# Four residual layers on one core: the down projection's rank products, moved into gate and up chunk by chunk and spread over the array's columns

## The reference, cut to what matters

```python
def lora_add(base, inp, A, B):                  # one adapter of rank 16 per batch
    t = einsum('bri,bni->bnr', A[idx], inp)
    return base + einsum('bor,bnr->bno', B[idx], t) * 0.5
gate = lora_add(einsum('bnh,fh->bnf', x, W_gate), x, A_gate, B_gate)     # f = 1376
up   = lora_add(einsum('bnh,fh->bnf', x, W_up),   x, A_up,   B_up)
act  = silu(gate) * up
down = lora_add(einsum('bnf,hf->bnh', act, W_down), act, A_down, B_down)
x = x + down
```

## Time and profile before

| | |
|---|---|
| time, median of 3 runs | 320.55 us (319.75 to 320.6) |
| profiled execution, its own time | 319.52 us |
| its span | 317.7 us |
| TensorE matmuls busy | 309.4 us (97%) |
| VectorE, ScalarE, GpSimd busy | 153.2, 107.0, 20.1 us |
| granted TensorE clock, mean | 0.999 |

### The profile page before, as it was taken

The page is one execution under the profiler, slowest core; times in us unless marked ns, Lnnn a source line. Parts: engine busy times, 40 slices in busy tenths (PEclk is TensorE's granted clock), DMA queues, the critical chain, the costliest instruction groups (busy, mean ns, idle before and its releaser), DMA issues.

```text
span 317.7 us, 4612 instructions
## 1 busy us (share of the span) xinstructions
PE 309.4 (97%) x1672; PEld 256.3 (81%) x1672; DVE 153.2 (48%) x250; ACT 107.0 (34%) x164; POOL 20.1 (6%) x25
## 2 busy tenths in 40 slices
PE   6879999999999999999999999999999999999996
PEld 5358788988888888888888888888889788897886
DVE  0198997967669437254254254255624431111101
ACT  1276562504445346243243243245325220000000
POOL 2086400200100000000000000000000000000000
PEclk9999999999999999999999999999999999999999
DMA  5989981015203400431431421550632002110111
GB/s 170 340 298 356 366 287 41 0 38 170 59 2 124 140 2 0 133 101 34 132 99 34 132 99 33 166 148 0 193 121 93 0 0 66 35 33 2 46 53 35
DMA packets 23888, 33.21 MB, mean 105 GB/s; under 512 B 3264, under 2 KB 16064, under 8 KB 23744
## 3 DMA queue, kind: packets, MB, share of 16 engines
q1 hardware_dynamic: 23584, 32.48, 32.0%
q10 hardware_dynamic: 288, 0.52, 0.5%
HBM read 30.89 MB, written 2.10 MB: 104 GB/s over the span
## 4 chain that ended last, share of the span: by engine, by line
PE 92%; SPq 3%; DMA 3%; POOL 1%; issue 1%; DVE 0%
PE bank L956 24%; PE bank L957 24%; PE bank L958 24%; PE bank L1101 3%; PE bank L1057 3%; DMA aw_raw<-in_aw 3%; PE bank L910 3%; PE bank L1003 2%; PE bank L940 1%; PE bank L890 1%; PE bank L942 1%; PE bank L941 1%; PE bank L932 1%; SPq L324 1%; SPq L304 1%; PE bank L1124 1%
## 5 line engine op out<-in xcount | busy, mean ns | idle before, releaser
L956 PE MATMUL bank<-xb,wgu_hl 128*128 128x512 f32 x176 | 69.1, 392 | 0.0
L957 PE MATMUL bank<-xb,wgu_hl 128*128 128x512 f32 x176 | 69.0, 392 | 0.0
L958 PE MATMUL bank<-xb,wgu_hl 128*128 128x512 f32 x176 | 68.5, 389 | 0.0
L958 PEld LDWEIGHTS bank<-xb,wgu_hl 128*128 128x128 f32 x176 | 33.1, 188 | 7.2
L815 DVE TENSOR_TENSOR act_f<-bank,act_f 128x512 f32<-128x512 f32 x22 | 15.2, 691 | 48.9 <-PE bank L1057 47.2
L956 PEld LDWEIGHTS bank<-xb,wgu_hl 128*128 128x128 f32 x176 | 33.0, 188 | 5.8
L957 PEld LDWEIGHTS bank<-xb,wgu_hl 128*128 128x128 f32 x176 | 33.2, 189 | 5.3
L956 PE MATMUL bank<-act_hl,wd_hl 128*128 128x512 f32 (+1 forms) x99 | 36.6, 370 | 0.0
L957 PE MATMUL bank<-act_hl,wd_hl 128*128 128x512 f32 (+1 forms) x99 | 36.2, 366 | 0.0
L958 PE MATMUL bank<-act_hl,wd_hl 128*128 128x512 f32 (+1 forms) x99 | 36.2, 366 | 0.0
L421 ACT ACTIVATE act_hl<-act_f 128x512 f32 (+1 forms) x22 | 13.9, 632 | 61.7 <-DVE act_f L815 61.6
(11 more groups left out here) (127 smaller groups left out, 450.5 us busy)
## 6 DMA issues: line engine op xcount, KB each, us to landing
w_raw<-in_w SPq DMA_DIRECT2D x22, 256.0 KB, 7.5
wgu_raw<-in_wgu SPq DMA_DIRECT2D x11, 512.0 KB, 3.4
bgu_raw<-in_bgu SPq DMA_DIRECT2D x88, 64.0 KB, 2.2
w_raw<-in_w SPq DMA_DIRECT2D x7, 512.0 KB, 7.4
out<-x_f SPq DMA_DIRECT2D x7, 256.0 KB, 2.4
x_f<-in_xT SPq DMA_DIRECT2D x6, 256.0 KB, 7.5
wd_own<-in_wd SPq DMA_DIRECT2D x2, 704.0 KB, 4.9
wd_raw<-in_wd SPq DMA_DIRECT2D x2, 704.0 KB, 4.3
```

Of the source, the lines that this page charges most:

```text
L956: pe.matmul(dst, w_hi, x[0][:, cols], start=start, stop=False)
L957: pe.matmul(dst, w_hi, x[1][:, cols], start=False, stop=False)
L958: return pe.matmul(dst, w_lo, x[0][:, cols], start=False, stop=stop)
```

## The change

The rank products of the down projection no longer form a block behind gate and up. `down_ranks(fc)` now does one chunk of both halves: for each half, four matmuls, one per batch, of plain float32 weights (`ad_raw`, 16 columns, no split) by plain float32 values (`act_f`, 128 columns), batch j of the half into partitions 32j to 32j+15 of bank h, which are the array's output columns from 32j on. Chunk fc-1 is done inside chunk fc, between gate and up of half 0, and the last chunk after the first piece of the down projection. The sums over chunks accumulate in bank 0 and bank 1, of which DVE first sets 128 columns to zero.

So the splitting of `ad`, `td_uv` and its splitting, and the two L1134 matmuls go. `td_copy` copies the banks' 128 columns to `td_sb`, and `spread_ranks(h)` makes two plain float32 matmuls of 128 columns with a selecting matrix `td_sel`, which POOL builds. ScalarE's silu of a chunk now also waits (`td_tm`) until the rank products of the chunk before have read `act_f`. `ad_raw` is loaded much earlier, into the place of layer 2's `a2_hl`. TensorE's loop over chunks 1 to 10 is written out. In the down projection the order of pieces and of the splits around them is new: both spreads stand after the second piece.

```diff
-        ad_raw = at("ad_raw", o_act + 80 * KB, [B, FC, R])
-        ad_hl = at("ad_hl", o_ad, [B, FC, 2, R], F32R)
+        ad_raw = at("ad_raw", o_ad, [B, FC, R])
         td_st = at("td_st", o_slot2 + 4 * KB, [T], F32R)
-        td_uv = [at(f"td_uv{i}", o_slot2 + 2 * i * KB, [HT], F32R) for i in range(H)]
+        td_sb = at("td_sb", o_ad + 8 * KB, [H, S])
+        td_sel = at("td_sel", o_ad + 9 * KB, [2, P])
...
+            sp.wait_ge(l2_tm, 2)
+            for b in range(B):
+                sp.dma_start(ad_raw[:, b], ad[adapter3[b]]).then_inc(ad_in, 16)
...
+            pool.memset(td_sel[:], 0.0).then_inc(td_sel_step, 1)
+            pool.wait_ge(td_sel_step, 1)
+            pool.wait_ge(sel_in, 16)
+            for j in range(HB):
+                rows = slice(32 * j, 32 * j + 32)
+                first = 64 * (j % 2)
+                pool.tensor_copy(td_sel[rows, j // 2, first:first + 64],
+                                 sel_raw[rows, 3 * P:3 * P + 64]).then_inc(td_sel_step, 1)
+            pool.wait_ge(td_sel_step, 1 + HB)
...
-            def td_uv_high(h):
-                act.wait_ge(td_tm, h + 1)
-                high(td_uv[h][0:2 * R], bank[h][0:2 * R]).then_inc(td_uv_hi, 1)
+            def td_copy(h):
+                act.wait_ge(td_tm, 2 * FC - 1 + h)
+                high(td_sb[:, h], bank[h][:, 0:S]).then_inc(td_copied, 1)
...
                         if h == 0:
                             act.wait_ge(act_lo, 2 * fc - 1)
+                            act.wait_ge(td_tm, 2 * fc - 1)
                         else:
                             act.wait_ge(act_lo, 2 * fc)
+                            act.wait_ge(td_tm, 2 * fc)
...
             act.wait_ge(up_done, 2 * FC)
             down_split_hi("wd_1")
             down_split_hi("bd")
-            act.wait_ge(act_lo, 2 * FC)
-            td_uv_high(0)
+            td_copy(0)
+            td_copy(1)
             down_split_hi("wd_2")
             td_high(0)
+            td_high(1)
             down_split_hi("wd_3")
-            td_uv_high(1)
...
+            def zero_td_bank(h):
+
+                dve.wait_ge(t3_uv_lo, h + 1)
+                dve.memset(bank[h][:, 0:S], 0.0).then_inc(td_banks_zeroed, 1)
...
             down_split_lo("bd")
-            td_uv_low(0)
             down_split_lo("wd_2")
             td_low(0)
+            td_low(1)
             down_split_lo("wd_3")
-            for i in range(C):
-                x3_add(i)
-            td_uv_low(1)
-            td_low(1)
-            for i in range(C, len(DOWN_PIECES)):
+            for i in range(len(DOWN_PIECES)):
                 x3_add(i)
 
 
...
-            with pe.Fori(0, (FC - 1) // 2) as i:
-                for u in range(2):
-                    fc = 2 * i + 1 + u
-                    slot = 1 - u
-                    pe.wait_ge(wgu_lo, fc + 1)
-                    pe.wait_ge(bgu_ready, fc + 1)
-                    for h in range(H):
-                        pe.wait_ge(silu_done, 2 * fc - 1 + h)
-                        gate_up_main(0, h, slot)
-                        gate_up_lora(0, h, slot)
-                        pe.wait_ge(act_mul, 2 * fc - 1 + h)
-                        gate_up_main(1, h, slot)
-                        gate_up_lora(1, h, slot)
-
-
-            def down_ranks(h):
-
-                pe.wait_ge(act_lo, 2 * FC - 1 + h)
-                for j in range(HB):
-                    b = HB * h + j
-                    for f in range(FC):
-                        for k in range(2):
-                            ins = pe.matmul(bank[h][0:2 * R, j * S:(j + 1) * S],
-                                            ad_hl[:, b, f].rearrange("p k r -> p (k r)"),
-                                            act_hl[:, f, k, b * S:(b + 1) * S],
-                                            start=(f == 0 and k == 0), stop=(f == FC - 1 and k == 1))
-                ins.then_inc(td_tm, 1)
+
+            def down_ranks(fc):
+
+                for h in range(H):
+                    pe.wait_ge(act_mul, 2 * fc + h + 1)
+                    for j in range(HB):
+                        ins = pe.matmul(bank[h][32 * j:32 * j + R, 0:S], ad_raw[:, HB * h + j, fc],
+                                        act_f[h][:, j * S:(j + 1) * S], start=(fc == 0), stop=(fc == FC - 1))
+                    ins.then_inc(td_tm, 1)
+
+            pe.wait_ge(ad_in, 16 * B)
+            pe.wait_ge(td_banks_zeroed, H)
+            for fc in range(1, FC):
+                slot = fc % 2
+                pe.wait_ge(wgu_lo, fc + 1)
+                pe.wait_ge(bgu_ready, fc + 1)
+                for h in range(H):
+                    pe.wait_ge(silu_done, 2 * fc - 1 + h)
+                    gate_up_main(0, h, slot)
+                    gate_up_lora(0, h, slot)
+                    if h == 0:
+                        down_ranks(fc - 1)
+                    pe.wait_ge(act_mul, 2 * fc - 1 + h)
+                    gate_up_main(1, h, slot)
...
+            def spread_ranks(h):
+
+                pe.wait_ge(td_copied, h + 1)
+                for q in range(2):
+                    ins = pe.matmul(bank[2 + h][:, q * S:(q + 1) * S], td_sel[:, q], td_sb[:, h], start=True,
+                                    stop=True)
+                ins.then_inc(td_done, 1)
+
+            pe.wait_ge(act_lo, 2 * FC - 1)
+            down_main(0, 0)
+            down_ranks(FC - 1)
+            down_main(0, 1)
+            pe.wait_ge(td_sel_step, 1 + HB)
             for h in range(H):
-                i = C * h
-                down_ranks(h)
-                down_main(h, i)
-                pe.wait_ge(td_uv_lo, h + 1)
-                pe.matmul(bank[2 + h][:], sel_r[0:4 * R, 3], td_uv[h][0:4 * R], start=True,
-                          stop=True).then_inc(td_done, 1)
-                down_main(h, i + 1)
-                pe.wait_ge(down_lo, down_nth["bd"])
-                pe.wait_ge(td_lo, 2 * h + 2)
+                spread_ranks(h)
+            down_main(0, 2)
+            pe.wait_ge(down_lo, down_nth["bd"])
+            pe.wait_ge(td_lo, 2)
+            for i in range(3):
                 down_lora(i)
-                down_lora(i + 1)
-                for i in range(C * h + 2, C if h == 0 else len(DOWN_PIECES)):
-                    down_main(h, i)
-                    down_lora(i)
+            down_main(0, 3)
+            down_lora(3)
+            pe.wait_ge(act_lo, 2 * FC)
+            pe.wait_ge(td_lo, 4)
+            for i in range(C, len(DOWN_PIECES)):
+                down_main(1, i)
+                down_lora(i)
 
 
 # ---- launch: one core; the host only lays the arrays out ----
```

More of the change, by code:

```diff
@@ L145, in bass_four_residual_layers @@
         sel_raw = at("sel_raw", o_slot2 + 5 * KB, [4 * P + 1])
-        sel_r = own("sel_r", [4, P], F32R)
+        sel_r = own("sel_r", [3, P], F32R)
         hi_lo = own("hi_lo", [1])
@@ L189, in bass_four_residual_layers @@
         t3_zeroed, td_zeroed = sem("t3_zeroed"), sem("td_zeroed")
+        td_sel_step, td_banks_zeroed = sem("td_sel_step"), sem("td_banks_zeroed")
         x0_hi, x0_lo, aw1_split = sem("x0_hi"), sem("x0_lo"), sem("aw1_split")
@@ L201, in bass_four_residual_layers @@
         x_hi, t2_hi, t3_uv_hi, t3_hi = sem("x_hi"), sem("t2_hi"), sem("t3_uv_hi"), sem("t3_hi")
-        sel_copied, t2_uv_hi, td_uv_hi = sem("sel_copied"), sem("t2_uv_hi"), sem("td_uv_hi")
+        sel_copied, t2_uv_hi, td_copied = sem("sel_copied"), sem("t2_uv_hi"), sem("td_copied")
         wgu_hi, bgu_hi, silu_done, act_hi = sem("wgu_hi"), sem("bgu_hi"), sem("silu_done"), sem("act_hi")
-        ad_hi, down_hi, td_hi = sem("ad_hi"), sem("down_hi"), sem("td_hi")
+        down_hi, td_hi = sem("down_hi"), sem("td_hi")
         w0_lo, x1_sum, x1_lo = sem("w0_lo"), sem("x1_sum"), sem("x1_lo")
@@ L211, in bass_four_residual_layers @@
         t2_lo, t3_uv_lo, t3_lo = sem("t2_lo"), sem("t3_uv_lo"), sem("t3_lo")
-        t2_uv_lo, td_uv_lo, hi_lo_copied = sem("t2_uv_lo"), sem("td_uv_lo"), sem("hi_lo_copied")
+        t2_uv_lo, hi_lo_copied = sem("t2_uv_lo"), sem("hi_lo_copied")
         wgu_lo, bgu_ready, act_mul, act_lo = sem("wgu_lo"), sem("bgu_ready"), sem("act_mul"), sem("act_lo")
-        ad_lo, down_lo, td_lo, x3_sum = sem("ad_lo"), sem("down_lo"), sem("td_lo"), sem("x3_sum")
+        down_lo, td_lo, x3_sum = sem("down_lo"), sem("td_lo"), sem("x3_sum")
         def w0_landed(b):
@@ L283, in td_block @@
             dst = td_st[rows, h * HT:(h + 1) * HT].rearrange("p (q b s) -> p q b s", b=2, s=S)
-            src = bank[2 + h][rows].rearrange("p (q b s) -> p q b s", b=2, s=S)
-            return dst[:, :, par], src[:, :, par]
+            src = bank[2 + h][rows, 0:2 * S].rearrange("p (q s) -> p q s", s=S)
+            return dst[:, :, par], src
         DOWN_PIECES = [(o, slice(h * HT, (h + 1) * HT)) for h in range(H) for o in range(C)][:-1]
@@ L367, in _ @@
             load_gate_up(FC - 1, 0)
-            for b in range(B):
-                sp.dma_start(ad_raw[:, b], ad[adapter3[b]]).then_inc(ad_in, 16)
```

(54 more changed lines are left out.)

## The result

| | before | changed |
|---|---|---|
| median | 320.58 us (319.64 to 321.13, 8 runs) | 317.57 us (315.61 to 319.06, 8 runs) |
| ratio to before, 95% interval | | 0.992 [0.9899, 0.9942] |
| profiled execution, span | 319.52, 317.7 us | 317.15, 315.3 us |

The change made the kernel 0.8% faster, between 1.9 and 3.2 us. The forecast was 324.7 us and slower. The time lies just inside the stated range, but on the other side of no change. That it lies inside is no merit of the forecast's case: the range reached down to 317.5 us only because rival 2 with dear switches, at a chance of 0.09, was let in.

A forecast was written before the change was run, and what follows sets the result against it. The prediction took TensorE's own instructions to bound the kernel. It summed 10.9 + 4.3 + 0.9 - 11.9 = +4.2 us onto 320.55 us, forecasting 324.7 us, with a range of 317.5 to 331.

The forecast's parts named there:

- rival 2: Rank products: four batches run at once, 4.8 us in all, giving 314.9 or 318.7 us by edge price; chance 0.21.
- dear switches: Each of 11 times in and out of the narrow columns costs TensorE 0.39 us, 4.3 us in all.
- What bounds the kernel: From 121 us on only TensorE's own instructions set the time; work taken from VectorE and ScalarE is worth nothing.
- Removed: On TensorE the two old rank blocks, 10.7 us, and the two L1134 matmuls, 1.2 us, go: 11.9 us.
- the spread: In the down projection, four full-array float32 matmuls of 128 columns, 8 instructions of 0.11 us, add 0.9 us.
- The new rank products: 176 instructions of 0.11 us in 11 blocks, partly overlapping between column groups, add 10.9 us.
- nine steps: A block of eight rank matmuls takes 9 steps of 0.11 us instead of 16, 0.99 us.
- In and out of the narrow columns: TensorE goes from full array to 32 columns and back 11 times, adding 4.3 us at 0.39 us each.
- the dear row: L1134, using 64 of the array's rows, cost 0.39 us more than a plain matmul; 11 times is 4.3 us.
- the cheap row: Behind the old rank block only 0.05 us were lost; 11 times is 0.6 us.
- Moved: Later waits, ad_raw's transfers, DVE's zeroings, the written-out loop and the last splits were costed at nothing.
- sixteen steps: Rank instructions run one after the other, 19.4 us in all, giving 329.5 or 333.3 us; chance 0.27.

The follow-up runs named there:

- the first experiment: The changed kernel with the four batches of a half all sent to the same 16 output columns and summed there; 331.53 us, ratio 1.0368 to the kernel before.
- the full-width weights: The one-group-of-columns kernel with 128 columns of ad_raw as stationary operand of each rank matmul; 327.89 us, ratio 1.026 to the kernel before.

## Why the prediction failed, point by point

**What bounds the kernel**: right. Only TensorE's starts counted; the splits that went from VectorE and ScalarE gave nothing.

**Removed, 11.9 us**, and **the spread, 0.9 us**: right as far as the profile after can say. The spread's eight instructions and the matmul behind them take 265.38 - 264.26 = 1.12 us, less 0.23:

```profile
264.26 1.05 PE L1139 MATMUL bank<-td_sb,td_sel 128*128 128x128 f32 x8
265.07 0.48 PE L964 MATMUL bank<-act_hl,wd_hl 128*128 128x512 f32 x1
265.38 0.40 PE L965 MATMUL bank<-act_hl,wd_hl 128*128 128x512 f32 x1
```

**The new rank products, 10.9 us: this is the step that failed.** Its instruction price of 0.11 us was right. The count of nine steps was wrong, and with it the argument "the second instruction of a matmul needs the columns that the first is still using, so it comes 0.11 us later; the first instruction of the next batch ... can go beside it". It supposed that an instruction which waits for its columns holds up all behind it. The order of starts was read from rows in which every matmul used the same columns, where no other order could show. In the changed kernel a block is four rounds, 11 x 0.44 = 4.8 us, the prediction's own lower end and its rival 2. The experiments with four and with eight in a row show what holds in its place: the groups of columns go their own way as long as no more than three instructions of a group are waiting (with three waiting the next group began, with more it did not). The Trainium skill ("TensorE: Matmul & The Clock Gate", Part 3: Packing small matmuls — row/col tiling) gives a factor of 2.38 for three groups; an estimate by it, 19.4 / 2.38 = 8.2 us, is nearer than my 10.9 and still too dear. Four groups gave a factor of 4.0 here, 1.76 to 0.44. The same section of the Trainium skill says that matmuls stay in program order in their starts and ends, which agreed with the nine steps. For the starts the experiment with four in a row contradicts it, and the measurement decides.

**In and out of the narrow columns, 4.3 us**: right that the price is paid, somewhat high in size. It measured 0.32 to 0.36 us a block, 3.5 to 4.0 us, where I had 0.39 from L1134. The choice of the dear row came out right partly by luck. L1134 uses half of the array's rows and all its columns, so its 0.39 is another case, and that the sizes lie close is not explained. Of the two reasons against the cheap row, that its matmuls all used the same columns is refuted by the first experiment. The other, its split kind, may be why it paid only 0.05, or its 32 columns instead of 16; no run separates them. Two blocks a chunk, two chunks a block and the full-width weights show the price of the new matmuls from three sides, +3.0, -2.4 and -3.5 us. The Trainium skill ("TensorEngine Tiling (Array Packing)", Key Properties) says that changing the tiling mode drains TensorE. These three runs agree with that; whether the old block, at 0.05 us, was such a change nothing here tells.

**Moved, at nothing**: held. No wait of TensorE on another engine appeared after 121 us. DVE's two zeroings took 0.30 us, and the only wait beside them is the 0.2 us of a weight load for t3_low, which was there before. ad_raw's eight transfers ran from 93.09 to 97.74 and pushed chunk 2's loads from 96.98 to 98.14, unseen. The last split of W_down ended at 269.56 and was needed at 273.36. The loop written out: no difference, by its own experiment.

**The sum with the measured terms.** Eleven blocks of 0.80 = 8.8, and 0.9, less 11.9: -2.2 us. The profiled executions differ by 2.4 us, the medians by 3.0, the ratio's interval by 1.9 to 3.2. Had only the rounds been right, the sum would have read 4.8 + 4.3 + 0.9 - 11.9 = -1.9 us, the case to which the prediction gave 0.09.

**The chances.** The cases were the right ones, but 0.79 of the chance lay on those with nine or sixteen steps, for no better reason than that the trace had no row with two groups of columns. For a resource that the trace never shows in use, the two ends deserved more nearly equal weight.

What stays open: why the old 32-column block paid so little at its edges and L1134 so much, and why the profiled edges of a new block are 0.32 us by one reading (pair to second matmul) and 0.36 by the other (pair to pair). The first matmuls just behind a block start 0.24 instead of 0.23 us apart, and nothing here explains that.

## What to carry to other kernels

Narrow plain float32 matmuls (16 columns here) in four groups of output columns ran four at a time: 16 instructions in 0.44 us, 4.8 us for all 176. The split kind in one group of columns ran one after the other at 60 ns each, 10.7 us for as many. Going in and out took back 3.5 to 4.0 us of that. Write such matmuls so that neighbours in the program use different columns: two or four instructions in a row for one group cost nothing here, eight in a row doubled the block. Gather them into few blocks, since each time in and out of the narrow columns cost 0.3 us for blocks of 8, 16 and 32 instructions alike. Doing two chunks at once took the ratio from 0.992 to 0.9845, and the gain between the medians from 3.0 to 4.7 us.

## What the runs showed of the hardware that was not expected

- Instructions for different groups of columns start out of the program's order. Sixteen, of which four in a row are for one group, are done in four rounds of 0.11 us.
- This reaches only so far: with eight in a row the next group began once the fifth had started and three were waiting, and a block of 32 took 2.54 instead of 1.20 us.
- The 32-column block of the kernel before, in the split kind, paid 0.05 us at its edges, the 16-column block in plain float32 0.32. The same plain float32 matmuls at full width paid nothing (0.03 us). Whether the kind or the width makes the first two differ is open.
